# Attention, two-way selective scan and top-half FFN on one core: a new split of the B scaling, no second SBUF tensor on VectorE, a hinted loop edge, and new places

## What is computed

```python
# 1: attention over the 1024 points of each image
attn = softmax((Wq x + bq)^T (Wk x + bk) * scale); x = attn (Wv x + bv) + x
# 2: a Mamba block, forwards and on the reversed tokens, over t = tokens(x)
xc, z = split(LN(t) @ in_proj)            # 256 + 256 columns (DI = 256)
xc = silu(causal_conv4(xc) + conv_b)
dt, Bm, Cm = split(xc @ x_proj)           # 16, 16, 16 (DS = 16)
dt = softplus(dt @ dt_proj + dt_b)
h[s] = exp(dt * A[s]) * h[s] + dt * Bm[s] * xc     # for each of 16 states s, along tokens
y = (sum_s h[s] * Cm[s] + xc * Dp) * silu(z) @ out_proj
m = y_forward + y_backward
t = t + m + leaky_relu(LN(m) @ w1 + b1) @ w2 + b2
# 3: an FFN (GELU) for the 511 tokens of highest weight of each image
w = LN(t) @ wr; y = FFN(LN(t)) * w where rank(w) < 511, else 0
t = t + LN(t) + y
```

## Time and profile before

| what | us |
|---|---|
| three runs, median (lowest to highest) | 8619.99 (8608.84 to 8632.47) |
| the profiled execution | 8629.83 |
| its span, first to last instruction | 8628.1 |
| busy in the span: PE, DVE, ACT, POOL | 7996.8, 7505.7, 7333.3, 7292.5 |

### The profile page before, as it was taken

One profiled execution on the slowest core, in us unless ns is written; L12 is line 12 of the kernel. 1 busy time (PEld: TensorE's weight loads), 2 busy tenths in 40 slices (PEclk: granted clock), 3 DMA queues, 4 the chain that ended last, 5 costly groups with the idle time before them and its releaser, 6 DMA issues. The chain is left out here.

```text
span 8628.1 us, 152387 instructions
## 1 busy us (share of the span) xinstructions
PE 7996.8 (93%) x53760; PEld 6192.3 (72%) x53760; DVE 7505.7 (87%) x10155; ACT 7333.3 (85%) x12894; POOL 7292.5 (85%) x5965
## 2 busy tenths in 40 slices
PE   6899999999999999999999999999999999999987
PEld 4777777777777777777777777777777777777765
DVE  3888998888998889998889899889988889998886
ACT  3888888888888888988888888889888889888875
POOL 2889888888888888888888888888888989888985
PEclk8999999999999999999999999999999999999998
DMA  1222222222222222222222222222222222222221
GB/s 41 72 65 77 73 73 74 64 72 75 72 75 68 68 73 75 75 71 70 66 73 75 73 73 67 71 71 76 73 70 66 76 70 75 75 72 65 76 71 37
DMA packets 321380, 604.48 MB, mean 70 GB/s; under 512 B 40961, under 2 KB 43714, under 8 KB 320578
## 3 DMA queue, kind: packets, MB, share of 16 engines
q1 hardware_dynamic: 320578, 594.31, 22.3%
HBM read 556.42 MB, written 20.97 MB: 67 GB/s over the span
## 5 line engine op out<-in xcount | busy, mean ns | idle before, releaser
L1049 POOL TENSOR_TENSOR g<-h,c_all 128x1024 f32<-128x1024 f32 x2048 | 4977.7, 2431 | 669.6 <-DVE h L1143 485.6
L841 ACT ACTIVATE da<-dt,a_neg 128x512 f32<-128x512 f32 x4096 | 2777.0, 712 | 117.7 <-DVE h L1143 114.1
L1143 DVE TENSOR_TENSOR_SCAN h<-da,h,ps 128x512 f32<-128x512 f32 x2048 | 2553.9, 1269 | 249.6 <-PE ps L511 113.4
L1143 DVE TENSOR_TENSOR_SCAN h<-da,ps 128x512 f32<-128x512 f32 x2048 | 2432.3, 1209 | 319.0 <-PE ps L511 191.4
L511 PE MATMUL ps<-ident,ub 128*128 128x128 f32 x16384 | 2410.9, 278 | 317.1 <-DVE h L1143 200.6
L511 PEld LDWEIGHTS ps<-ident,ub 128*128 128x128 f32 x16384 | 1896.5, 142 | 1039.4 <-issue 545.3
L853 ACT ACTIVATE ub<-u_tok,b_tok 128x256 f32<-128x256 f32 x5120 | 2247.9, 497 | 131.2 <-PE ps L511 60.8
L515 PE MATMUL ps<-ident,g 128*128 128x128 f32 x16384 | 2284.1, 275 | 7.3 <-POOL g L1049 7.3
L515 PEld LDWEIGHTS ps<-ident,g 128*128 128x128 f32 x16384 | 1907.9, 142 | 459.3 <-issue 448.9
L1035 POOL TENSOR_SCALAR ub<-u_tok,b_tok 128x256 f32<-128x256 f32 x3072 | 1539.8, 511 | 398.6 <-DVE u_tok L1231 211.7
L830 ACT ACT_TABLE_LOAD x476 | 610.7, 1283 | 8.5
(11 more groups left out here) (123 smaller groups left out, 9269.2 us busy)
## 6 DMA issues: line engine op xcount, KB each, us to landing
c_all<-c_rows SPq DMA_DIRECT2D x2048, 256.0 KB, 3.2
x_in<-in_x SPq DMA_DIRECT2D x32, 512.0 KB, 5.2
t_old<-t SPq DMA_DIRECT2D x32, 512.0 KB, 3.2
out<-tile_b SPq DMA_DIRECT2D x32, 512.0 KB, 4.1
c_rows<-rows SPq DMA_DIRECT2D x128, 32.0 KB, 2.8
w_conv<-in_conv_rows SPq DMA_DIRECT2D x1, 512.0 KB
f_w<-in_f_w SPq DMA_DIRECT2D x2, 256.0 KB
hid<-in_in_proj SPq DMA_DIRECT2D x1, 256.0 KB
```

The lines of the kernel that those rows point to most:

```text
L841: act.activation(da[:, n % 2, half, :], dt[:, slot, half, :], ACT.Exp, scale=a_neg[:, r, half, s:s + 1]).then_inc(da_made, 1)
L1049: pool.tensor_tensor(g[:, n % 2, :, :], h[:, n % 2, :, at:at + BANK], c_all[:, n % RING, :].unsqueeze(1).to_broadcast([P, NH, BANK]), ALU.mult
L1143: dve.tensor_tensor_scan(h[:, n % 2, half, at:at + BANK], da[:, n % 2, half, :], ps[:, DB + half, :], before, ALU.mult, ALU.add).then_inc( ...
```

## The change

- Places: nearly all tables are new. Attention of the next image stretches from place 137 to 182 for its last `t1`; LN 1 and the MLP move from the places 136 to 158 to the places 182 to 199, and the ranks from 202 to 217 to 230 to 239.
- `scale_u`: ScalarE and GpSimd make two blocks each in every step.
- VectorE has no instruction with two tensors from SBUF: the taps accumulate in the PSUM bank of the projection; the maximum of `dt` and `u` read and write the banks Y, and ScalarE then copies `dt` to SBUF (AT_DTKEEP), for which TensorE's turning of `u` and ScalarE's `decay` wait; the leaky step on VectorE takes `max(x + b1, hid)`, where ScalarE has put `0.01 * (x + b1)` into `hid`; `tied` compares a copy of the weights in which GpSimd has set later tokens to the lowest number (`earlier`, one selection over 1024 columns an image); `w_kept` is a threshold on VectorE and a product on GpSimd.
- ScalarE's copy of the turned probabilities stands ahead of the exponential of the same place, and in the first turn a place earlier.
- The loop is built with a hint of its back edge.

```diff
-    AT_ROWKEEP = (35, 106, 166, 223)
-    AT_DTMAX = (51, 118, 180, 241)
-    AT_U = (54, 120, 181, 243)
-    AT_UT = (54, 120, 180, 243)
-    AT_UKEEP = (57, 122, 184, 246)
-    AT_CSTORE = (44, 97, 179, 220)
+    AT_ROWKEEP = (28, 95, 164, 213)
+    AT_DTMAX = (47, 117, 182, 223)
+    AT_U = (51, 118, 183, 226)
+    AT_DTKEEP = (51, 116, 180, 231)
+    AT_UT = (49, 118, 183, 239)
+    AT_UKEEP = (54, 122, 186, 242)
+    AT_CSTORE = (22, 114, 171, 212)
...
-    AT_RANK = (202, 205, 205, 209, 209, 209, 212, 217)
-    AT_WK = 223
+    AT_EARLIER = 223
+    AT_RANK = (230, 231, 231, 232, 234, 234, 234, 239)
+    AT_WK = 240
+    AT_WTIMES = 237
...
-    AT_T3 = (224, 245)
+    AT_T3 = (243, 247)
-    AT_STORE = 251
+    AT_STORE = 244
-    FIRST_PTKEEP = tuple(FIRST + 5 + 4 * i for i in range(8))
+    FIRST_PTKEEP = tuple(FIRST + 4 + 4 * i for i in range(8))
...
                         if at == AT_UT[k]:
-                            pe.wait_ge(u_made, since(u_made, prep(k, 1, 1)))
+                            pe.wait_ge(dt_kept, since(dt_kept, prep(k, 1, 1)))
...
                             elif c == 0:
-                                pe.wait_ge(hid1_kept, since(hid1_kept, o))
+                                pe.wait_ge(hid1_leaky, since(hid1_leaky, o))
...
-                        for b in range(QB // 2 + n % 2):
+                        for b in range(QB // 2):
                             t = act.activation(ub[:, n % 2, b, :], u_tok[:, slot, b, :], ACT.Copy,
                                                scale=b_tok[:, slot, b, s:s + 1])
...
-                            act.activation(xc[:, slot, 1, :], ps[:, Y + 1, :], ACT.Identity, bias=conv_b[:, r, 1:2],
+                            act.activation(ps[:, Y + 1, :], ps[:, Y + 1, :], ACT.Identity, bias=conv_b[:, r, 1:2],
                                            scale=w_taps[:, r, PAD:PAD + 1]).then_inc(proj_kept, 1)
...
+                        if at == AT_DTKEEP[k]:
+                            act.wait_ge(u_made, since(u_made, prep(k, 1, 1)))
+                            act.activation(dt[:, side, :, :], ps[:, Y:Y + NH, :], ACT.Copy).then_inc(dt_kept, 1)
...
-                            act.activation(hid[:, o, :], banks(X), ACT.Identity, bias=b1[:, o:o + 1]
+                            act.activation(hid[:, o, :], banks(X), ACT.Identity, bias=b1_low[:, o:o + 1], scale=SLOPE
                                            ).then_inc(hid1_kept, 1)
...
-                        for b in range(QB // 2 + n % 2, QB):
+                        for b in range(QB // 2, QB):
                             t = pool.tensor_scalar(ub[:, n % 2, b, :], u_tok[:, slot, b, :],
                                                    b_tok[:, slot, b, s:s + 1], 1.0, ALU.mult, ALU.mult)
...
+                            if at == AT_EARLIER:
+
+                                pool.wait_ge(w_row_kept, since(w_row_kept, 1))
+                                pool.wait_ge(base_made, since(base_made, 2))
+                                pool.affine_select(out=by_block(earlier), in_=by_block(w_row[:, :]), compare_op=ALU.is_gt,
+                                                   fill=LOWEST, base=0, pattern=[[0, NB], [-1, P]], channel_multiplier=1
+                                                   ).then_inc(earlier_made, 1)
+                            if at == AT_WTIMES:
+                                pool.wait_ge(ranked, since(ranked, 1))
+                                pool.tensor_tensor(w_kept[:], is_kept[:], w_col[:], ALU.mult).then_inc(w_kept_made, 1)
...
-                            dve.scalar_tensor_tensor(xc[:, slot, 1, :], x_proj[:, slot % NCH, tap:tap + BANK],
-                                                     w_taps[:, r, tap:tap + 1], xc[:, slot, 1, :],
+                            dve.scalar_tensor_tensor(ps[:, Y + 1, :], x_proj[:, slot % NCH, tap:tap + BANK],
+                                                     w_taps[:, r, tap:tap + 1], ps[:, Y + 1, :],
                                                      ALU.mult, ALU.add).then_inc(tapped, 1)
...
-                                dve.scalar_tensor_tensor(dt[:, side, half, :], ps[:, Y + half, :],
+                                dve.scalar_tensor_tensor(ps[:, Y + half, :], ps[:, Y + half, :],
                                                          b_dt[:, r, half:half + 1], dt[:, side, half, :],
-                                                         ALU.add, ALU.max).then_inc(dt_kept, 1)
+                                                         ALU.add, ALU.max).then_inc(dt_max, 1)
...
-                            dve.tensor_tensor(u[:], dt[:, side, :, :], xc[:, slot, :, :], ALU.mult).then_inc(u_made, 1)
+                            dve.tensor_tensor(u[:], ps[:, Y:Y + NH, :], xc[:, slot, :, :], ALU.mult).then_inc(u_made, 1)
...
-                            dve.scalar_tensor_tensor(hid[:, o, :], hid[:, o, :], SLOPE, hid[:, o, :],
-                                                     ALU.mult, ALU.max).then_inc(hid1_leaky, 1)
+                            dve.scalar_tensor_tensor(hid[:, o, :], banks(X), b1[:, o:o + 1], hid[:, o, :],
+                                                     ALU.add, ALU.max).then_inc(hid1_leaky, 1)
...
-                            dve.scalar_tensor_tensor(tied[:, j % 2, :], w_row[:, mine], w_col[:, j:j + 1], below[:],
-                                                     ALU.is_equal, ALU.mult, accum_out=heavier[:, 2, j:j + 1]
-                                                     ).then_inc(counted, 1)
+                            dve.tensor_scalar(tied[:, j % 2, :], earlier[:, mine], w_col[:, j:j + 1], None,
+                                              ALU.is_equal, ALU.add, accum_out=heavier[:, 2, j:j + 1]).then_inc(counted, 1)
...
-                            dve.scalar_tensor_tensor(w_kept[:], rank[:], float(KEPT), w_col[:], ALU.is_lt, ALU.mult
-                                                     ).then_inc(w_kept_made, 1)
+                            dve.tensor_scalar(is_kept[:], rank[:], float(KEPT), None, ALU.is_lt).then_inc(ranked, 1)
...
-        with nc.Fori(0, (B - 2) // JOINED) as group:
+        with nc.Fori(0, (B - 2) // JOINED, hint_back_edge=True) as group:
```

More of the change, by code:

```diff
@@ new lines, in conv_attn_mamba_mod_kernel @@
+    AT_T1 = (50, 61, 83, 110, 120, 133, 153, 182)
+    LN_STATS = {0: (131, 194), 1: (15, 30), 2: (211, 213)}
+    LN_AGGR = {0: (154, 195), 1: (16, 44), 2: (212, 213)}
+    LN_POW = {0: 192, 1: 48, 2: 211}
+    LN_APPLY = {0: (197, 197), 1: (58, 67), 2: (216, 216)}
+    LN_TURN = {0: 199, 1: 182, 2: 217}
+    LN_KEEP = {0: 201, 1: 180, 2: 217}
+    AT_MT = (24, 30)
+    AT_B2 = (29, 68)
+    AT_T1OLD = 38
+    AT_W1 = (184, 185, 189, 189)
+    AT_HID1 = (184, 190)
+    AT_LEAKY = (191, 195)
+    AT_W2 = (195, 195, 195, 195)
@@ L241, in conv_attn_mamba_mod_kernel @@
         m_normed, n2 = by_block(tile_a[:, :]), by_block(tile_a[:, :])
+        earlier = tile_a[:, :]
         n2c, out_s = tile_b[:, :], tile_b[:, :]
@@ L308, in _ @@
                 pool.memset(heavier[:], 0.0)
[L309 removed]
+                pool.wait_ge(zeroed, 1)
                 pool.affine_select(out=ident[:], in_=ident[:], compare_op=ALU.not_equal, fill=1.0,
[L311 to L312 removed]
                                    base=0, pattern=[[-1, P]], channel_multiplier=1)
@@ L324, in _ @@
                 dve.tensor_scalar(bq[:], bq[:], SCALE, None, ALU.mult)
+                dve.tensor_scalar(b1_low[:], b1[:], SLOPE, None, ALU.mult)
                 dve.tensor_copy(wr_cols[:], wr[:].to_broadcast([C, P]))
@@ new lines, in conv_attn_mamba_mod_kernel @@
+            (ln_turned[2], 1), (ln_var[0], 8), (ln_var[1], 8), (ln_var[2], 8), (m_kept, 4), (m_made, 4),
+            (max_made, 8), (mlp_made, 2), (mt_made, 2), (out_kept, 1), (out_turned, 1), (probs_kept, 8),
+            (probs_made, 8), (probs_turned, 8), (proj_kept, 8), (proj_made, 4), (q_kept, 1), (q_made, 1),
+            (ranked, 1), (rinv_made, 8), (rows_kept, 4), (rows_made, 4), (scores_made, 8), (stored, 16),
+            (summed, 1), (t1_made, 8), (t1_moved, 16), (t2_made, 1), (t3_made, 8), (tapped, 12), (u_kept, 4),
@@ L875, in prepare @@
                             act.wait_ge(proj_made, since(proj_made, prep(k, 1, 1)))
-                            if k == QUARTERS - 2 and last:
-                                act.wait_ge(m_made, since(m_made, closing(0, 1, 1)))
-                            if k == QUARTERS - 1 and now:
-                                act.wait_ge(m_made, since(m_made, closing(1, 1, 1)))
                             if k >= 2 and now or joined:
@@ L954, in attend_next @@
                             act.activation(v_tok[:], blocks(X), ACT.Copy).then_inc(v_kept, 1)
+                        for i in due(at_ptkeep, at):
+                            act.wait_ge(probs_turned, since(probs_turned, i + 1))
+                            if i:
+                                act.wait_ge(attn_made, since(attn_made, i))
```

(1 more changed line is left out.)

144 lines of the change are left out of this document (62 added, 82 removed).

## The result

The changed kernel takes 8358.5 us (median of 4 runs, 8355.4 to 8358.9) against 8614.4 before (median of 4, 8604.4 to 8632.5). The ratio is 0.970, with a 95% interval of 0.968 to 0.972: faster by 3.0%.

What follows compares the result with a forecast made beforehand. No single engine but the loop of scan, transposition and next scan was taken to bound the kernel. Terms -100 + 38 + 0 - 18 - 8 = -88 took 8620 to 8530 us, range 8360 to 8790.

Steps and rivals of the forecast that it cites:

- Step 1: VectorE without second SBUF tensors: 107 us of stalls gone, threshold taken as unstalled, 100 us counted as time saved.
- rival B: Stalls did more harm than they last, as a shut-out shifts both queues: 8406 us, chance 0.16.
- step 2: GpSimd gets back 121 us on g and 59 on ub, together 180 us of its busy time.
- Step 3: New split of ub: GpSimd's load 7641 us, net +377, of which a tenth, 38 us, counts as time lost.
- Step 4: dt via PSUM: copy's cost and ScalarE's relief cancel, bounds -100 and +134; leaky step covered, 39 us if not.
- rival C: The copy in dt's chain lies on the path: 8664 us, chance 0.05.
- Step 5: Loop's back edge with the hint: five taken edges save 18 us, bound 0.
- Step 6: Head: copy of turned probabilities ahead of the next exponential saves 1.1 us for seven blocks, 8 us; bound 0.
- Step 7: Queue waits on SP and GpSimd: GpSimd's wait for ranked some 3.5 us, costed at zero, bound 112 us.
- Step 8: New places: priced by no row, said to decide how much of the other terms is path, counted in the range only.

Runs made afterwards that it cites:

- e10: Changed kernel with only the taps back on two SBUF tensors: 8816.1 us, 1.021 of the kernel before.
- e3: Kernel before with the new split and every new place, but VectorE's old forms, no copy of dt and no hint: 9033.0 us, 1.049.
- e8: Changed kernel with GpSimd's product w_kept at place 241 instead of 237, behind g of that step: 8356.7 us, 0.968 of the kernel before.
- e17: Kernel before, at its old places and split, with only the new taps, tied and head order: 8496.3 us, 0.984.
- e14: Kernel before at old places with the new split, head order, taps, leaky step, tied and w_kept; old dt and u, no hint: 8756.3 us, 1.015.
- e15: Changed kernel at the old places and with the old split, new forms and hint kept: 8984.7 us, 1.041 of the kernel before.
- e4: Changed kernel at the places of the kernel before, new forms, split and hint kept: 8983.6 us, 1.043 of the kernel before.
- e7: Changed kernel without the back-edge hint: 8373.0 us, 0.970 of the kernel before.
- e5: Kernel before with only the back-edge hint added: 8629.4 us, 1.000.
- e6: Kernel before with only the new places; old forms, old split, no hint: 8821.6 us, 1.022.
- e11: Changed kernel with dt back in SBUF, the old maximum and u, and no copy: 8550.9 us, 0.991 of the kernel before.

## Why the prediction was right or wrong

**What bounds.** The reading held as far as it was tested. At the new places long stalls in VectorE's queue came out as time nearly one for one (459 us for 458 in e10, 643 for 660 in e3), and GpSimd at 92% did not bound. Not every stall counts: 15 us more for the threshold in e8 cost nothing.

**Step 1 and 2, stalls: right in kind, too small.** For taps and `tied` I had 60 us of durations. At the old places the measured gain is 106 (e17), 24 more than the 82 by which VectorE's busy time fell; that surplus goes the way of rival B, and what makes it isn't shown. At the new places the form of the taps alone, which I put at 3 us, is worth 458 (e10): I had read the stalls where the old order put them. GpSimd's `g` and `ub` got faster as in step 2. I costed the threshold as unstalled because of its form. It is unstalled, but only because GpSimd stands waiting for it; the form is shut out like the others (e8).

**Step 3, split: failed.** I had +38 everywhere. It measured +145, +211, +114, 0 and -46, by what else is in the kernel. The tenth of the net load was a guess about slack that the places decide: at the old ones scans wait 163 us for `g` (e14), at the new ones 101, and there the split gains. The load itself was mis-sized too: GpSimd is busy 7462 us in the stretch, 179 below my 7641, mostly because its other instructions shortened as well (84 us, step 2 left them out) and `ub` and `earlier` cost some 60 us less than I had.

**Step 4, `dt` and the leaky step: failed, in both ways.** I took 0 within -100 and +134 for `dt`. At the old places it cost 342 us with the old split and 227 with the new one, since I had priced the copy's duration and not the turning, keeping and scaling that wait behind it (the waits of e15 and e4): rival C, at up to two and a half times its price. At the new places the same form is 192 us better than the old one. The leaky step cost 109 at the old places where I allowed 39: once in each image, as I had it, but 3.4 us and not 1.22, since one late matmul also holds back the transposition of `ub` behind it in TensorE's queue.

**Step 5: right for this kernel**, 16 us of the 18 (e7), though under 10 at the old places (e5).

**Step 6: mis-sized**, 26 instead of 8. No run has the new order of the head alone, but every run that has it starts its first scan at 133 to 137 us, and every run without it at 157 to 163. I had counted the copy's 1.1 us in each block of the first turn. A block takes 6.5 us, where its exponentials stood 10.3 us apart before (from 60.67 to 112.12 us, five blocks). The two kernels' rows of one block each, TensorE's product with V, before and after:

```profile
72.24 2.67 PE L508 MATMUL ps<-v_tok,probs_t 128*128 128x128 f32 x16 [2.59 <-ACT probs_t L966]
...
75.42 3.78 PE L508 MATMUL ps<-k_all,q 128*128 128x512 f32 x4 [0.51 <-DVE t L1299]
```

```profile
63.62 2.05 PE L515 MATMUL ps<-v_tok,probs_t 128*128 128x128 f32 x16 [1.11 <-ACT probs_t L966]
...
66.18 1.98 PE L515 MATMUL ps<-k_all,q 128*128 128x512 f32 x4 [0.51 <-DVE t L1315]
```

The same matmuls are shorter, with a higher granted clock (below).

**Step 7: `ranked` right in the time** (zero, e8), though the wait is 249 us or 7.8 an image where I had 3.5; but `w_kept`'s way over GpSimd, costed at nothing, was 37 us at the old places (e17).

**Step 8 is the step that failed most.** "All are new, and no row prices them", and so they counted in the range only. In fact they carry the result: from e4 to the changed kernel is 625 us, with every form and the split the same. And they carry it only with the forms: with the old ones they lose 2.2% (e6). Two things in that could be seen in advance, as I read it now. The diff's places could have been counted for table loads: ScalarE's switches follow from the tables alone (476 against 352; an estimated 113 us). And at the old places VectorE's two-tensor instructions mostly miss `g` (taps at 0.750 in the median); at the new ones they don't (1.9 us a tap in the mean, if the forms are old). An order that may put a tap beside `g` has more freedom, which the new forms give; that this freedom is what the new tables use is argued, not shown. Of the 625 us, some 420 hang on the way of `dt` (e4, e14, e11 and the changed kernel); the other 205 or so the new places also give with the old `dt`. How those 205 divide between the table loads (an estimated 113), the leaky step, `w_kept` and the hint stays open: a mix of old and new tables was not tried. Which of the moved places relieves the chain of `dt` stays open too.

**Why the total came out at 1.0%:** the sum's parts were priced at the old places. There the whole change without its new places is not 1.0% faster but 4.3% slower (e4), and the best part of it tried there is 1.6% faster (e17). So the forecast was right in its sign by luck: what made the kernel faster was the term that it put at nothing.

## What to carry to other kernels

In a kernel whose order is written out by hand, forms and places are one change: a form that looks free is priced by where it stands, so test each form with the order made for it, and the order with the forms it was made for. A wait is priced by what stands behind it in its queue, up to the next scan, not by its own length. Count what the order itself decides, table loads for one, before calling it "not priced".

## What the runs showed of the hardware that was not expected

**The clock in the head.** Windows from 60 to 100 us, before and after:

```profile
60.00:100.00 40.00, 28.36 (x111) 19.88 (x110) 5.99 (x12) 8.48 (x12) 0.00 (x0) 0.74 0.00 0
```

```profile
60.00:100.00 40.00, 27.11 (x164) 19.77 (x162) 10.67 (x32) 11.63 (x16) 1.34 (x3) 1.00 0.00 1
```

The granted clock was 0.74, a mix of the 1.2 and 2.4 GHz levels, with TensorE idle 2.3 to 2.6 us ahead of each product with V; in the changed kernel it is 1.00, the upper level, in this window, and that idleness is 1.1 us. Moving a copy ahead of an exponential of 1.1 us in ScalarE's queue goes with 26 us less ahead of the first scan.

**Writing PSUM costs VectorE next to nothing here.** A tap that reads and writes PSUM takes 0.725 us at least, one into SBUF 0.718.

**The selection over 1024 columns** takes GpSimd 1.093 us, where the estimate from the slope was 1.68.
